# A 1024-step GRU with narrower recurrent products: two columns in place of 20 and 40

## The reference

```python
def step(h, xs):
    xzt, xrt, xht = xs
    z = jax.nn.sigmoid(xzt + h @ U_z + vz)
    r = jax.nn.sigmoid(xrt + h @ U_r + vr)
    hh = jnp.tanh(xht + r * h @ U + vh)
    h_new = (1.0 - z) * h + z * hh
    return (h_new, h_new)
```

## Time and profile before

| what | us |
|---|---|
| median of 3 runs (lowest, highest) | 1880.47 (1879.51, 1880.57) |
| the profiled execution | 1878.24 |
| its span, first to last instruction | 1876.4 |
| TensorE busy | 1844.4 (98%) |
| VectorE busy | 1454.8 (78%) |
| ScalarE busy | 713.4 (38%) |
| GpSimd busy | 199.4 (11%) |
| mean granted TensorE clock | 0.999 |

### The profile page before, as it was taken

How to read it: one execution, slowest core, us unless ns; L and a number is a source line. 1 busy time by engine, 2 the same in 40 slices (tenths; PEclk the granted TensorE clock), 3 DMA queues, 4 the chain that set the end, 5 groups by cost and what they waited for, 6 DMA issues and landing times.

```text
span 1876.4 us, 101766 instructions
## 1 busy us (share of the span) xinstructions
PE 1844.4 (98%) x39969; PEld 1703.9 (91%) x39970; DVE 1454.8 (78%) x11505; ACT 713.4 (38%) x3785; POOL 199.4 (11%) x515
## 2 busy tenths in 40 slices
PE   8999999999999999999999999999999999999998
PEld 8998999989899998999989999899999989999766
DVE  5787878778787787877878787787877878788776
ACT  4333433434333343433434344343433434334322
POOL 0110101101020110101101011110101101011000
PEclk9999999999999999999999999999999999999999
DMA  9000000000000000000000000000000000000000
GB/s 321 4 4 5 5 4 5 5 4 5 5 5 5 4 5 5 4 5 5 4 5 5 4 5 5 4 5 5 4 5 5 4 5 5 5 5 4 5 5 4
DMA packets 16926, 23.62 MB, mean 13 GB/s; under 512 B 3585, under 2 KB 15160, under 8 KB 16445
## 3 DMA queue, kind: packets, MB, share of 16 engines
q1 hardware_dynamic: 15280, 17.05, 2.6%
q10 hardware_dynamic: 1164, 0.07, 0.0%
HBM read 15.01 MB, written 2.10 MB: 9 GB/s over the span
## 4 chain that ended last, share of the span: by engine, by line
PE 94%; DVE 2%; ACT 2%; issue 1%; ACTq 0%; DVEq 0%
PE up_ps L740 20%; PE y_ps L758 20%; PE r_ps L863 13%; PE c_ps L863 13%; PE r_ps L842 6%; PE z_ps L863 6%; PE c_ps L842 5%; PE z_ps L872 4%; ACT rc_tanh_ps L408 2%; PE y_ps L690 2%; DVE h_cur L662 1%; PE c_ps L774 1%; PE z_ps L774 1%; DVE p_cur L633 1%; PE r_ps L774 1%
## 5 line engine op out<-in xcount | busy, mean ns | idle before, releaser
L740 PE MATMUL up_ps<-feat,up_w 128*128 128x128 f32 x2528 | 519.2, 302 | 0.2
L758 PE MATMUL y_ps<-hidden,down_w 128*128 128x128 f32 x2528 | 515.4, 301 | 0.0
L839 PEld LDWEIGHTS <-u_high 128*128 128x128 f16 x4096 | 398.2, 97 | 20.7
L408 ACT ACTIVATE rc_tanh_ps<-r_ps 128x4 f32<-128x4 f32 x1024 | 161.8, 158 | 574.5 <-PE r_ps L863 574.4
L740 PEld LDWEIGHTS up_ps<-feat,up_w 128*128 128x128 f32 x2528 | 362.3, 190 | 1.2 <-ACT hidden L397 0.9
L758 PEld LDWEIGHTS y_ps<-hidden,down_w 128*128 128x128 f32 x2528 | 360.4, 190 | 0.0
L863 PEld LDWEIGHTS r_ps<-h_cur,u_mid 128*128 128x128 f16 x4096 | 252.1, 96 | 113.6 <-issue 46.6
L863 PE MATMUL c_ps<-p_cur,u_mid 128*128 128x40 bf16 (+10 forms) x4096 | 337.4, 179 | 0.0
L863 PE MATMUL r_ps<-h_cur,u_mid 128*128 128x20 bf16 (+5 forms) x4096 | 336.4, 178 | 0.0
L662 DVE TENSOR_TENSOR_SCAN h_cur<-rc_tanh_ps,blend 128x8 f32<-128x8 f32 x1024 | 178.0, 174 | 165.5 <-ACT rc_tanh_ps L408 165.4
L288 POOL TENSOR_TENSOR hidden<-hidden,expert_w 128x128 f32<-128x128 f32 (+3 forms) x416 | 163.9, 394 | 1339.0 <-ACT hidden L397 1339.0
(11 more groups left out here) (154 smaller groups left out, 4059.0 us busy)
## 6 DMA issues: line engine op xcount, KB each, us to landing
up_w<-in_L_cond_ew SPq DMA_DIRECT2D x4, 1024.0 KB, 9.3
down_w<-in_L_cond_ew SPq DMA_DIRECT2D x4, 1024.0 KB, 10.4
x_rows<-in_x SPq DMA_DIRECT2D x8, 256.0 KB, 4.6
out<-out_rows SPq DMA_DIRECT2D x128, 16.0 KB, 1.8
up_w<-in_L_cond_sw SPq DMA_DIRECT2D x1, 1024.0 KB, 12.7
down_w<-in_L_cond_sw SPq DMA_DIRECT2D x1, 1024.0 KB, 13.4
cf<-in_L_cond_C_r SPq DMA_DIRECT2D x1, 256.0 KB, 9.6
cf<-in_L_cond_C_z SPq DMA_DIRECT2D x1, 256.0 KB, 9.4
```

The source lines that it names most:

```text
L408: act.activation((tanh_r, tanh_z, c_now)[g].rearrange("p (m b) -> p m b", b=B), before_tanh, ACT.Tanh, scale=0.5 / GAIN).then_inc(act_done, 1)
L740: last = mm(up_ps[n % 2][:, 0:COLS], up_w[:, e, k, j * P:(j + 1) * P], feat[:, k, c * COLS:(c + 1) * COLS], start=(k == 0), stop=(k == KC ...
L758: last = mm(y_ps[:, m * COLS:(m + 1) * COLS], down_w[:, e, j, m * P:(m + 1) * P], hidden[:, n % TILES_HELD, :], start=False, stop=(m == KC ...
L839: pe.ldweights(w[:, g, k, m * P:(m + 1) * P])
```

## The change

All recurrent products stream the columns with data alone: 2, and 4 in `recur_two`. The four buffers shrink to that size.

```diff
-FILL = 40
-H_FILL = 20
+FILL = 2
+H_FILL = 2
...
                 at = (c % 2) * REGION + m * COLS + (t - 1) * B
-                width = 2 * B if last_of_sum else min(H_FILL, RANK - at)
+                width = 2 * B
```

## The result

2615.06 us median (2614.94 to 2615.32) against 1880.39 us: a ratio of 1.391, interval 1.389 to 1.392. The kernel is 735 us slower, where I had forecast 34 us and a range up to 1990 us.

What follows compares the result with a forecast made beforehand. It took a chain round the engines, 1.77 us a step, to bound the kernel. Narrower products gave 0; falls at filler steps 3.5 + 28 us and a few elsewhere 3 us, together 34: 1880.5 + 34 = 1914 us, range 1888 to 1990 us.

Steps and rivals of the forecast that it cites:

- Part 1: Recurrent products of every step: narrowing them at the full clock changes nothing, 0 us, 2 us either way.
- Part 2: Filler steps of the last chunk and two knots in each other chunk: the clock falls there, together 34 us.
- Ordinary narrow steps hold, mostly: Steps with feed-forward or projection work: mostly keep the full clock; falls at filler steps alone had chance 0.53.
- close to a step that fell: Ordinary steps after the change: 0.73 us of streaming a step, against 0.68 us in the step that fell.
- The fall seen ended by itself after 3.4 us. If falls and returns alternate: Last chunk's 64 filler steps: half of 115 us low, 17 falls x 0.2 = 3.5 us.
- the one of constant falling: Rival, all ordinary steps: 3.4 us low and high alternate, 2105 to 2125 us; mostly or always had chance 0.14.
- What a fall costs: Per fall: about 0.85 us beside work (0.7 to 1.1), 0.2 us in filler steps (0.1 to 0.3).
- The filler step's 0.1 us: Filler steps at the low clock: each pays about 0.1 us for its two fillers of 384 columns and latency.
- The rival from the page: Whole kernel: no pause in TensorE's work, so the clock stays full and time 1880.5 us; no change had chance 0.05.

Runs made afterwards that it cites:

- burst kernel: Kernel after plus 60 fillers of 384 columns after step t = 8 of each of the first 15 chunks: 2231.7 us.
- spell kernel: Kernel before with narrow products only in steps t = 16 to 39 of the even chunks (the narrow spells): 1879.9 us.
- the one with narrow knots: Kernel before with narrow products only in t = 0 to 2 and t = 56 to 63 of the first 15 chunks: 1975.9 us, ratio 1.050.
- 12 of 15 chunks: Kernel before with narrow products only in t = 3 to 55 of the first 15 chunks: 2007.6 us, ratio 1.067.

## Why the prediction was wrong

- **Part 1, narrow products at the full clock cost and gain nothing:** right. Steps at 1.00 take 1.775 us in the kernel after (there is one whole such step), in the burst kernel and in the narrow spells, and the spell kernel's time is that of before.
- **Part 2, filler steps fall:** right at the end of a chunk (a "knot" of filler steps), in all 29 that the burst kernel (14) and the one with narrow knots (15) reached at 1.00. The first fall came even earlier than I looked for it, at t = 2, where one filler still stands in place of work.
- **Ordinary narrow steps hold, mostly:** right when the clock is up: 14 of 15, 8 of 8 and 12 of 15 chunks. The four that fell all the same fit "close to a step that fell" (0.73 against 0.68 us).
- **"The fall seen ended by itself after 3.4 us. If falls and returns alternate":** this is the step that failed. The one fall in the trace of before was followed by steps with 20 and 40 columns. I carried its length over to narrow steps, where nothing in the trace spoke for it, and all my cases, the one of constant falling too, were built on it. The runs show two lasting states: ordinary narrow steps mostly keep 1.00 where it is and always kept 0.50 where it was; in the kernel after the one fall lasted 2555 us, to the end. At the low clock the same 1704 columns of a step come in 2.59 us instead of 1.775, so TensorE does less in a given time. That this lengthening keeps the clock down is my reading; a clock that by itself rises less readily than it falls would look the same, and no run tells the two apart. Shown is only that wide steps, a burst, and some filler stretches bring the clock back, and ordinary narrow steps never did in these runs.
- **What a fall costs**, the second term that was off: 0.85 us a fall of some 1.45 steps is 0.6 us a step; measured 0.81. I had priced it on two steps with eight fp32 passes and two fillers of 384 columns between them; two ordinary steps have twelve passes. I had also let narrow products keep 0.025 us at the low clock; they have 0.027, and 0.07 behind the first of a block. The filler step's 0.1 us was right (1.86 to 1.88 against 1.78 us).
- **The rival from the page** (third in the list of rivals, though the prediction calls it the second) said no pause, no fall, and 1880.5 us. The Trainium skill, "TensorE: Matmul & The Clock Gate", section "Why this matters for your kernels", also tells to keep TensorE busy without a break to reach the full rate. The windows above show records busy for 2391 of 2391 us at 0.50. Busy in the profile's sense was neither enough to keep the clock nor to bring it back.

A small slip changes nothing: narrow, the recurrent products of a step stream 72 columns, not 80 (the four z products with `u_mid` take 2 each, not 4), so 736 columns are lost and not 728, 318 of them in r and z.

Both terms were needed. One fall at the start, 15 x 60 steps at the prediction's own 0.6 us and 0.1 us for each of some 120 filler steps would have been about 550 us; with the measured 0.81 us it is 740 us.

**Open:** why chunks 2, 4 and 6 fell and the others did not, which a shift in time might decide; why narrow steps cannot raise the clock; and why the step of two words out of every eight costs what it does, which was not measured apart from the recurrence.

## What to carry to other kernels

Where matmuls start at the same spacing whatever their width (here 0.025 us), more columns can be free, and can be what holds TensorE's clock; look for them before calling them waste, and find the width at which they begin to cost (here between 40 and 56, for the scattered operand between 20 and 56). Before pricing a fall of the clock, ask what would raise it again in the steps that follow, not how long the last one lasted: a fall that the work can't end costs for the rest of the kernel. Such a loss need not have a slope: with 30 columns for c it was 8 us, with 20 it was 502.

## What the runs showed of the hardware

- Two lasting levels under the same instructions: narrow steps ran at 1.00 for up to 53 steps in a row (94 us) and at 0.50 for 1000 and more.
- At the low clock the second narrow product of a block starts 0.07 us after the first, the others 0.027 us apart; at the full clock all are 0.025 us apart.
- Products of 56 columns are 0.026 to 0.027 us from start to start when they read `p_cur` word after word, and 0.053 to 0.054 us when they read two words out of every eight in `h_cur`.
